# An attention and mixture-of-experts block on one core: indirect scatters spread over pairs, the first group's loads moved up, the router moved behind the scores

## What is computed

```python
h = patches(x) @ W + b + pos_emb                 # 32 images, 16 patch tokens each, width 192
h = concatenate([h, txt], axis=1)                # 48 tokens an image: N = 1536 rows
h = h + attention(layernorm(h))                  # 12 heads of 16, rope on q and k, causal
xf = layernorm(h)
probs = softmax(xf @ gate_w.T)                   # 8 experts, top 2, weights renormalised
pos  = cumsum(onehot(top_i)) - 1                 # place of each row in its expert's buffer
buf[e * 480 + pos] = xf                          # 480 places an expert, later rows dropped
y = buf + silu(z @ w1) * (z @ w3) @ w2           # z = rms-normalised 2 * buf, per expert
out = h + weighted sum of each row's two y rows
```

## Time and profile before

| | |
|---|---|
| median of 3 runs | 343.22 us (343.16 to 345.55) |
| the profiled execution's own time | 339.86 us |
| its span, first to last instruction | 337.6 us |
| PE busy, mean granted clock | 268.4 us (79%), 0.886 |
| DVE / ACT / POOL busy | 168.5 / 134.8 / 118.7 us |
| attention pairs, first to last `shift` | 38.17 to 168.33 us |
| expert stage | from about 203 us to the end |

### The profile page before, as it was taken

How to read it: one execution, slowest core, us unless ns; L and a number is a source line. 1 busy time by engine, 2 the same in 40 slices (tenths; PEclk the granted TensorE clock), 3 DMA queues, 4 the chain that set the end, 5 groups by cost and what they waited for, 6 DMA issues and landing times.

```text
span 337.6 us, 5941 instructions
## 1 busy us (share of the span) xinstructions
PE 268.4 (79%) x2078; PEld 221.6 (66%) x2079; DVE 168.5 (50%) x497; ACT 134.8 (40%) x323; POOL 118.7 (35%) x132
## 2 busy tenths in 40 slices
PE   7028978898975998877855399999999999999920
PEld 3017866786864776575644147989898898989910
DVE  7222365676655657153646425554638274664210
ACT  0022457756662556336321215353434526352210
POOL 7212123222445213710257600072433517163451
PEclk9656999999998979758985579999999999999975
DMA  8900029910001100110011290466585758570322
GB/s 226 268 18 0 14 45 389 222 38 4 1 27 51 37 2 1 63 49 0 3 37 37 70 250 1 130 132 176 88 207 95 197 113 159 141 135 8 36 23 22
DMA packets 24398, 29.64 MB, mean 88 GB/s; under 512 B 3409, under 2 KB 21363, under 8 KB 24243
## 3 DMA queue, kind: packets, MB, share of 16 engines
q1 hardware_dynamic: 17043, 19.93, 22.4%
q0 software_dynamic: 5904, 8.48, 12.4%
q10 hardware_dynamic: 1424, 0.89, 1.1%
HBM read 18.87 MB, written 10.08 MB: 86 GB/s over the span
## 4 chain that ended last, share of the span: by engine, by line
PE 53%; DVE 11%; ACT 10%; issue 10%; DMA 6%; another core or an unknown queue 5%; POOL 3%; ACTq 0%; DVEq 0%; POOLq 0%; SPq 0%
PE bank L659 12%; PE bank L470 4%; ACT kbd L716 3%; PE bank L643 3%; PE bank L644 3%; PE bank L637 3%; PE bank L640 3%; PE bank L636 3%; DMA zs<-slots 3%; PE bank L399 2%; DMA h_all<-ptok_sb 2%; PE bank L409 2%; PE bank L431 2%; PE bank L432 2%
## 5 line engine op out<-in xcount | busy, mean ns | idle before, releaser
L1229 POOL DMA_INDIRECT out_rows<-yw,tok x32 | 51.3, 1604 | 87.0 <-ACT yw L836 79.6
L659 PE MATMUL bank<-w_sb,zero_sb 128*120 128x192 f32 x256 | 43.4, 328 | 1.1 <-DVE zero_sb L1107 1.0
L659 PEld LDWEIGHTS bank<-w_sb,zero_sb 128*120 128x120 f32 x256 | 41.4, 183 | 2.2 <-issue 2.1
L1107 DVE TENSOR_TENSOR zero_sb<-zero_sb,bank 128x480 f32<-128x480 f32 x32 | 20.8, 649 | 33.6 <-ACT zero_sb L827 33.6
L827 ACT ACTIVATE zero_sb<-bank 128x480 f32<-128x480 f32 x32 | 18.3, 571 | 31.0 <-PE bank L644 31.0
L755 ACT COPY oT<-bank 128x96 f32<-128x96 f32 (+1 forms) x32 | 5.9, 235 | 54.2 <-PE bank L505 36.6
L836 ACT ACTIVATE yw<-zero_sb,zs 120x192 f32<-120x192 f32 x32 | 12.8, 448 | 36.0 <-DVE zero_sb L1119 36.0
L1181 POOL DMA_INDIRECT slots<-rows,slot x24 | 24.0, 1001 | 8.4 <-issue 7.0
L636 PE MATMUL bank<-z0h,wah 128*128 128x480 f32 x64 | 25.3, 395 | 0.4 <-ACT z0h L812 0.4
L643 PE MATMUL bank<-z,wbh 128*128 128x480 f32 x64 | 24.4, 381 | 0.3 <-DVE z L1099 0.3
L640 PE MATMUL bank<-z0l,wah 128*128 128x480 f32 x64 | 24.4, 381 | 0.0
(11 more groups left out here) (141 smaller groups left out, 602.2 us busy)
## 6 DMA issues: line engine op xcount, KB each, us to landing
rawa_sb<-in_w SPq DMA_DIRECT2D x8, 512.0 KB
rawb_sb<-in_w SPq DMA_DIRECT2D x16, 256.0 KB
w_sb<-in_w SPq DMA_DIRECT2D x8, 384.0 KB
slots<-zero_sb POOLq DMA_DIRECT2D x1, 3030.0 KB
zs<-slots SPq DMA_DIRECT2D x8, 378.8 KB
patch_sb<-in_patches SPq DMA_DIRECT2D x1, 1152.0 KB, 11.8
out_rows<-h_all SPq DMA_DIRECT2D x4, 288.0 KB, 3.3
h_all<-in_txt ACTq DMA_DIRECT2D x7, 96.0 KB, 8.1
```

Source lines behind the costliest of these rows:

```text
L659: mm = pe.matmul(bank[6 + c // 2][0:CR, (c % 2) * D:(c % 2 + 1) * D], hT[:, m, c * CR:(c + 1) * CR], w2_sb[:, par, m, :], start=(m == 0), ...
L1107: dve.tensor_tensor(hT[:, m, :], sg[:, m % 2, :], bank[2 * (m % 2) + 1][:, 0:CAP], ALU.mult).then_inc(s_hT, 1)
L1229: pool.indirect_dma_start(out=out, out_offset=bass.IndirectOffsetOnAxis(ap=tok[:, e, c:c + 1], axis=0), in_=yw[:, c, :], in_offset=None, b ...
```

## The change

Five things, in one diff. **Router and scatters:** the batches become (0,1,2), (3,4,5), (6,7), (8), (9), (10), (11); `dispatch` takes one tile (two scatters) and has a pair of its own, `slot_of_dispatch`; `route1` now stands a pair later, in the pair `slot_of_route`, and both `route1` and `route2` behind `shift` in DVE's list; PE's `positions` writes to bank 7, so the projection waits for `route2`'s first two steps. **q and k:** the products of a group's three tiles stand in pairs 1, 2, 3 of four in place of 1, 2, 4, with their turning one pair later, and `turn_qk` stands ahead of the values' product on PE. **ACT's order:** the exponential before `copy_v`, the probabilities' copies before all copies of k. **Start:** ACT queues only the first group's part of the text at once; SP queues the other groups' patches and text after tile 0's tokens are in place; the clearing of `kbd` stands behind the first `patch_tokens`; ACT makes one dummy exponential early; PE has more idle matmuls (8 and 5 before the first turning, 2, 2 and 3 at pair 16). **DVE and POOL order:** `attention` is now first after `choose`, `norm1` ahead of rope, and the next tile's statistics at the end of a pair.

```diff
 def slot_of_qk_product(T):
-    return 4 * (T // TPG - 1) + (1, 2, 4)[T % TPG]
+    return max(0, 4 * (T // TPG - 1) + 1 + T % TPG)
 def slot_of_qk_transposes(T):
-    return max(0, 4 * (T // TPG - 1) + (2, 3, 5)[T % TPG])
+    if T < TPG:
+        return T - 1
+    return 4 * (T // TPG - 1) + 2 + T % TPG
-BATCHES = [(0, 1, 2), (3, 4, 5), (6, 7, 8), (9, 10), (11,)]
+BATCHES = [(0, 1, 2), (3, 4, 5), (6, 7), (8,), (9,), (10,), (11,)]
+def slot_of_route(n):
+    return slot_of_gate(BATCHES[n][-1]) + 1
+def slot_of_dispatch(T):
+    n = [T in b for b in BATCHES].index(True)
+    return slot_of_route(n) + 1 + BATCHES[n].index(T)
...
 @block.sync
+            sp.wait_ge(s_place[0], 48)
             sp.dma_start(patch_sb[:, :, P:4 * P], patches[:, :, P:4 * P]).then_inc(s_patch_rest, 16)
+            load_text(sp, slice(1, GROUPS), [s_txt_rest] * TPG)
...
 @block.tensor
             def project(T):
+                if done["positions"]:
+                    pe.wait_ge(s_r2, R2_STEPS * (done["positions"] - 1) + 2)
...
+            pe.wait_ge(s_ptok, 1)
+            stay_warm(8)
+            pe.wait_ge(s_place[0], 48)
+            stay_warm(5)
             turn_xn(0)
...
 @block.scalar
-            act.wait_ge(s_tokw, 16)
+            load_text(act, slice(0, 1), s_txt)
+            act.wait_ge(s_idle, 1)
+            act.activation(mx[:, 0:1], idle_sb[:, 0:1], ACT.Exp)
...
+                if i < NS:
+                    exponential(i)
                 if i + 1 < NS:
                     copy_v(i + 1)
-                if i < NS:
-                    exponential(i)
...
 @block.vector
-            dve.memset(kbd[:, :, :, :], 0.0).then_inc(s_ones, 1)
...
             patch_tokens(0)
+            dve.memset(kbd[:, :, :, :], 0.0).then_inc(s_ones, 1)
             statistics1(0)
...
-                for n in range(NB - 2):
-                    if slot_of_gate(BATCHES[n][-1]) + 1 == i:
-                        route1(n)
-                    if slot_of_gate(BATCHES[n][-1]) + 2 == i:
-                        route2(n)
...
                     shift(i)
...
+                for n in range(NB):
+                    if slot_of_route(n) + 1 == i and i < NS:
+                        route2(n)
+                    if slot_of_route(n) == i and i < NS:
+                        route1(n)
...
 @block.gpsimd
-            def dispatch(n):
+            def dispatch(T):
+                n = [T in b for b in BATCHES].index(True)
+                t = BATCHES[n].index(T)
                 pool.wait_ge(s_slot, n + 1)
                 pool.wait_ge(s_rms, n + 1)
-                for t, T in enumerate(BATCHES[n]):
-                    for k in range(2):
+                for k in range(2):
...
```

More of the change, by code:

```diff
@@ L307, in build, with load_text @@
         h_by_group = h_all[:, :, :].rearrange("p (g t) d -> p g t d", t=TPG)
+        def load_text(eng, groups, done):
+            pieces = []
+            for b in range(8):
+                lo = b * S + NPATCH
+                while lo < (b + 1) * S:
+                    hi = min((b + 1) * S, lo // P * P + P)
+                    pieces.append((lo // P, lo % P, b, lo - b * S - NPATCH, hi - lo))
+                    lo = hi
+            assert [sum(p[0] == t for p in pieces) for t in range(TPG)] == [3, 3, 3]
+            for t, at, b, s0, n in pieces:
+                eng.dma_start(h_by_group[at:at + n, groups, t, :],
+                              txt.rearrange("(g b) s d -> b s g d", b=8)[b, s0:s0 + n, groups, :]).then_inc(done[t], 16)
         @block.sync
@@ L578, in _ @@
                     scores(i)
+                for T in range(1, NT):
+                    if slot_of_qk_transposes(T) == i:
+                        turn_qk(T)
                 if i + 1 < NS:
@@ L607, in _ @@
                         gate_product(T)
[L608 to L612, removed]
                 if i == NS:
-                    positions(NB - 2)
+                    positions(NB - 3)
+                    stay_warm(3)
+            positions(NB - 2)
             positions(NB - 1)
@@ L799, in _ @@
                         copy_xT(T)
-                for n in range(NB - 2):
-                    if slot_of_gate(BATCHES[n][-1]) + 1 == i:
+                for T in range(1, NT):
+                    if slot_of_qk_transposes(T) == i:
+                        copy_k(T, range(4))
+                        copy_q(T)
+                for n in range(NB):
+                    if slot_of_route(n) == i and i < NS:
                         ratios(n)
-                if i == NS:
-                    ratios(NB - 2)
+            ratios(NB - 2)
             ratios(NB - 1)
@@ L1049, in _ @@
                     dve.tensor_copy(order_sb[:, :], orderf_sb[:, :]).then_inc(s_order, 1)
-                for T in range(TPG, NT):
+                    statistics1(TPG)
+                for n in range(NB):
+                    if slot_of_route(n) + 1 == i and i < NS:
+                        route2(n)
+                    if slot_of_route(n) == i and i < NS:
+                        route1(n)
+                if i == NS:
+                    route1(NB - 3)
+                for T in range(TPG + 1, NT):
                     if slot_of_first_transposes(T) == i:
-                        statistics1(T)
+                        norm1(T)
                 for T in range(2, NT):
@@ L1055, in _ @@
                         rope_parts(T)
-                for T in range(TPG, NT):
-                    if slot_of_first_transposes(T) == i:
-                        norm1(T)
+                if i == 0:
+                    norm1(TPG)
                 for T in range(NT):
@@ L1061, in _ @@
                         residual(T)
+                for T in range(TPG + 1, NT):
+                    if slot_of_first_transposes(T) == i + 1:
+                        statistics1(T)
             choose(NT - 2)
+            norm2(NT - 1)
+            route2(NB - 3)
             route1(NB - 2)
-            norm2(NT - 1)
+            choose(NT - 1)
             route2(NB - 2)
-            choose(NT - 1)
             route1(NB - 1)
@@ L1194, in _ @@
             for i in range(NS + 1):
-                for T in range(TPG, NT):
-                    if slot_of_first_transposes(T) == i:
-                        rstd_first(T)
+                if i == 0:
+                    rstd_first(TPG)
                 for T in range(2, NT):
@@ L1203, in _ @@
                         rstd_second(T)
+                for T in range(TPG + 1, NT):
+                    if slot_of_first_transposes(T) == i + 1:
+                        rstd_first(T)
                 if i == 0:
```

81 lines of the change are left out of this document (34 added, 47 removed).

## The result

The changed kernel takes 325.69 us (median of 4 runs, 325.46 to 326.69) against 344.29 (343.16 to 345.55) for the kernel before on the same chip: ratio 0.9465 [0.9416, 0.9513], 18.6 us less. The forecast was 318, range 306 to 331. The profiled executions are 325.46 (span 323.7) and 339.86 (span 337.6).

The account below looks back on a forecast made before the run. No engine bounds the whole: start loads, a PE, DVE, ACT, PE ring of 16 pairs, router's tail, experts. Start -9, holds -15.3, two scatters +6.3, order -5, tail -2 gave -25: 315 profiled, 318 median, range 306 to 331.

Parts of the forecast that it names:

- layernorm earlier: At the start: earlier bias step and quicker placing DMAs let the first layernorm start at 13.4 instead of 19.0, -5.6 us.
- clock at the start: PE's first products: 3 to 3.8 us back if 13 idle matmuls keep the high level, nothing if not; taken as -2.5.
- late patch load, text beside it: At the start: patches of groups 1 to 3 issued late, +0.5 (0 to +2); text beside first patches 0 (to +2.2).
- two scatters a pair: Pairs with two scatters: 0.9 us charged for late division in each of seven, +6.3; bounds 0 and 15.
- tail: Router's tail: tile 11's scatters at once, -2.3; one more batch +2.3; third train's hold partly gone; net -2 (-4 to +1).
- The start: Everything up to the pairs: layernorm, table load, clock and late load together, -9 us (from -6 to -11).
- The holds: Pairs 7 and 11: six scatters in a row hold DVE and ACT; idle 8.3, late divisions 2, low clock 5.0: -15.3.
- rival 2: Two scatters in a pair cost nothing and the start warms fully: -35, 308 us; chance 0.23.
- rival 3: Any scatter issued as PE passes from values to scores holds: 5.2 plus 2.5 low clock in eight pairs, 373; chance 0.05.
- Rival 1: Each pair of scatters holds 1.9 us in each of eight pairs, order gains nothing: 332; chance 0.2, shared with rival 4.
- Order: In the pairs: router behind the shift -1 in two pairs, exponential -3, third q and k product moved 0: -5.
- the exponential's -3: ACT's exponential, begun 0.4 us after the shift ended, comes earlier in perhaps half of the pairs: -3 us.

Follow-up runs that it names:

- experiment 4: Changed kernel with 12 and 16 idle matmuls in place of 8 and 5 before the first turning, first chip: 315.24 us, ratio 0.9494 to the kernel before.
- experiment 11: Changed kernel with SP queuing the other groups' patches and text without waiting for tile 0's tokens, third chip: 321.5 us, ratio 0.9703 to the kernel before.
- experiment 7: Kernel before with only the scatters spread, each tile's two in a pair of their own, second chip: 339.96 us, ratio 0.9915 to the kernel before.
- experiment 1: Changed kernel with a batch's scatters all in one pair again (trains of 6, 6, 4, 2), first chip: 321.97 us, ratio 0.9686 to the kernel before.
- experiment 10: Changed kernel with trains of six scatters, as in experiment 1, on the third chip: 321.02 us, ratio 0.9723 to the kernel before.
- experiment 6: Changed kernel, unchanged, run again as a control on the second chip: 323.62 us, ratio 0.9435 to the kernel before.
- experiment 8: Changed kernel with the edits of experiments 3 and 4 together, second chip: 313.89 us, ratio 0.9145 to the kernel before.
- experiment 2: Changed kernel with all 24 scatters behind pair 15, none in the pairs, first chip: 342.6 us, ratio 1.03 to the kernel before.
- experiment 3: Changed kernel with ACT's k and q copies for tiles 1 and 2 at the head of pairs 0 and 1, first chip: 314.24 us, ratio 0.9474.
- experiment 9: Changed kernel with positions, route1 and route2 back in front of attention and shift, third chip: 322.94 us, ratio 0.9724 to the kernel before.
- experiment 5: Kernel before, unchanged, run again with a profile as a control on the second chip: 344.42 us, ratio 1.0032.

## Why the prediction was right, and where it was not

The sign and the likeliest mechanism held, and 325.69 stands inside the range, 7.7 above the forecast. The forecast of 318 carried 25 us of gain over from the profiled execution. The medians show 18.6, but the two profiled executions only 14.4 (325.46 against the 315 forecast on their scale), so 7.7 is the kinder figure of the miss. Point by point, in the prediction's own terms:

| Term | forecast | measured | from |
|---|---|---|---|
| layernorm earlier | -5.6 | -5.2 | 18.99 to 13.82 |
| table load | -1.3 | -1.3 | load at 4.99, under PE |
| clock at the start | -2.5 | +1.4 | 4.04 for 3.30 and 1.49 for 0.82; experiment 4 gets 4.0 to 4.8 |
| late patch load, text beside it | +0.5 | 0 | load lands near 19, wanted at 22.77 |
| pairs 4 to 14: holds, two scatters, order in them | -14 | -15.7 | timelines |
| two scatters a pair | +6.3 | +4.9 to +5.5 / 0 | by chip: 53.4 to 53.9 / 48.5 |
| pairs 0 to 3: move of q and k, ACT's order | about 0 (-2 to +3) | +8.45 | 31.55 to 40.00 |
| tail | -2 | -0.8 | 25.33 to 24.52 |

(-14 is -15.3 + 6.3 - 5; the row on two scatters is a part of it.) **The start** gained 5.1 of the 9, and nothing beyond the layernorm. The step that failed is "if the 13 idle matmuls keep the high level": they did not, since PE stood still for 1.11 us between the two sets and for 2.26 before the first turning, and the clock was at its lower level from about 14.6 to 28. Twenty-eight matmuls, with a gap of 0.24 between the sets and none before the first turning, kept it. Number and gaps changed together, so which of them did it is not separated. What the wait on SP costs and hides was right: taking it away loses 3.3 us (experiment 11).

**The holds** went. Pairs 7 and 11, 11.10 and 12.39, now take 8.23 and 8.53. The step "if the six scatters in a row are what holds" is borne out where the kernel before takes 344: in experiment 7 there is no train at pairs 7 and 11 and no hold, and a train of four with one new hold. It is not the whole condition, since beside the trains at the end of the pairs ACT's copy came on time. And it is wrong as a rule for any chip: on two others a train of six held nothing (experiments 1 and 10). On its size there are two checks. On one chip, experiment 7's pairs 7 to 12 gained 11.3, with four pairs of scatters in them; my 15.3, less 0.9 for each of the four, would be 11.7. Across chips the kernel before is 11 to 13 us faster where nothing is held.

**Two scatters** cost 4.9 to 5.5 in all where the holds exist (result, experiments 6 and 8 against 2, 3 and 4), near the 6.3 that I took from the late first divisions, and nothing elsewhere, which is rival 2's price. The nearness is partly luck: some 2 of the 5.2 to 5.5 are the low clock in pair 13, which my term did not hold and rival 3 did. Rival 1's, 15, was never seen. Rival 3's 5.2 in each pair with scatters was not seen either: the dearest, pair 13, takes 8.31 against 6.24 without them.

**Order** is the term that was mis-sized most, and with the start's clock the reason that the forecast is 7.7 too low. I had written that "moving the third q and k product ... net 0" and counted -5 in all. I looked at which pair the turnings go to, and at what DVE's list and PE's list hold. I did not follow ACT's five copies of group 0, which the same edit moves behind `copy_pT`. They are wanted by the next scores in pairs 0 and 1: +7.0 by experiment 3, with the low clock behind, and 1.4 more that experiment 3 does not return (32.9 for pairs 0 to 3, against 31.55 before) and no run explains. How much of the exponential's -3 came can't be told from the holds: pairs 4 to 14 gained 15.7 net of 5.2 for the scatters, so holds and order together gave 20.9 there (forecast 20.3). For the router behind the scores I had counted -2. In the new order it is worth 5 by medians and 6.7 by the profiles (experiment 9): its place in front costs a wait for ACT's ratio of 2.33 in pair 6 and 2.31 in pair 10, and the steps behind it in four pairs.

**The tail** has the size that it was given, less 1.2. Tile 11's numbers are early, but the queue on POOL in front of them is not shorter.

Where nothing is held the changed kernel itself was not run. An estimate from the medians there: experiment 3's 314.24 plus 7.0, experiment 4's 315.24 plus 4.0 to 4.8, experiment 11's 321.50 less 3.3 to 3.8, so 318 to 321. Beside 332.5 and 331.5 that is 11 to 14 us of gain, against 18.6 and 19.9 where the holds exist. That the forecast of 318 comes near it is chance: the forecast had the holds in it, and neither ACT's copies nor the cold start.

**Left open.** What in the chip holds PE's results while POOL issues indirect DMAs, why some trains don't do it, and why it is absent on two of the chips. In the expert stage of the kernel before such DMAs run beside PE as well, and ACT follows in its usual 0.66.

## What to carry to other kernels

When an edit gathers or moves the copies that turn one stage's result over to the next, write down for the first and the last group, too, which instruction reads them next; a rule that gives slack in the later groups gave none in the first two pairs, and cost 7 us where 25 of gain were forecast. A train of indirect DMAs on one queue costs at least what stands behind it (here `rstd_second`, 1.46 us), and on some chips it can hold up the engines that read PE's results as well, so spread it as far as the tail allows and no further: all of it at the end left PE idle for 27.67 us in place of 4.42. Look at the granted clock behind idle matmuls before you count on them: here 13 with gaps of 1.11 and 2.26 us did not hold it up to the first real work, and 28 with a gap of 0.24 did.

## What the runs showed of the hardware that was not expected

- The same kernel took 331.5 and 332.5 us on two chips and 343.5 and 344.3 in the other two series. Where it took 343 to 344, idle times with the release "remote" stand while POOL issues indirect DMAs, 24.1 us added up over DVE and ACT in one execution; where it took 332 it has no profile, so that the difference lies there is inferred. In the held pairs ACT's copy of the turned attention goes on only when the train is out: 0.80 us after four scatters (experiment 7), 1.18 and 1.24 after six (experiment 5: 106.59 after 105.41, 144.60 after 143.36). Beside the trains at the end of the pairs it follows PE by 0.04.
- With two scatters in a row the delay is shorter and shows as a late wait for PE: DVE's division begins 1.50 us after the product's end in pair 9 and 1.04 in pair 12, against 0.05 in pair 9 on the chip without it.
- Thirteen idle matmuls in two sets, with 1.11 us between them and 2.26 behind, left the granted clock at 0.52 over 14 to 28. Twenty-eight, the last of which ended at 15.78, as the first turning began at 15.67, left it at 1.00.
